# Routing arithmetic woven into the attention's maxima, GpSimd's biases regrouped, and a last group finished tile by tile

## The reference

```python
xn = layernorm(x)
q, k, v = split(xn @ w_qkv.T)                       # 2048 x 128 each
attn = (softmax(q @ k.T / sqrt(8)) @ v) @ w_proj.T + b_proj
t = xn @ W_in + b_in
topv, topi = top_k(softmax(t @ W_gate + b_gate), 2) # 8 experts, gates normalised to sum 1
moe = sum over the two experts: gate * (relu(t @ W1[e] + b1[e]) @ W2[e] + b2[e])
out = x + attn + (moe @ W_out + b_out)
```

## Time and profile before

| what | us |
|---|---|
| median of 3 runs | 242.5 |
| lowest and highest | 242.16, 242.7 |
| profiled execution, its own time | 242.35 |
| its span, first to last instruction | 240.6 |
| TensorE busy in the span | 226.1 (94%) |
| VectorE, ScalarE, GpSimd busy | 136.6, 111.7, 140.9 |

### The profile page before, as it was taken

How to read it: one execution, slowest core, us unless ns; L and a number is a source line. 1 busy time by engine, 2 the same in 40 slices (tenths; PEclk the granted TensorE clock), 3 DMA queues, 4 the chain that set the end, 5 groups by cost and what they waited for, 6 DMA issues and landing times.

```text
span 240.6 us, 4828 instructions
## 1 busy us (share of the span) xinstructions
PE 226.1 (94%) x1724; PEld 214.0 (89%) x1724; DVE 136.6 (57%) x330; ACT 111.7 (46%) x265; POOL 140.9 (59%) x163
## 2 busy tenths in 40 slices
PE   7699977999999999899999999999899999999983
PEld 7688865889999998899999999999899899999983
DVE  4978585364252551445444445444677886985642
ACT  2572520433524325354444554444656656567561
POOL 3149007888888820266555666553088888888610
PEclk9999999999999999999999999999999999999999
DMA  6799911101111121022222222221111113113201
GB/s 180 282 324 341 322 31 46 45 33 46 46 41 39 43 66 44 14 55 76 70 73 71 67 71 75 69 75 38 33 46 34 44 35 82 40 40 83 75 15 44
DMA packets 23047, 19.54 MB, mean 81 GB/s; under 512 B 3280, under 2 KB 19696, under 8 KB 22768
## 3 DMA queue, kind: packets, MB, share of 16 engines
q1 hardware_dynamic: 20000, 14.71, 20.1%
q0 software_dynamic: 2048, 4.20, 6.5%
q10 hardware_dynamic: 976, 0.33, 0.5%
HBM read 10.97 MB, written 8.26 MB: 80 GB/s over the span
## 4 chain that ended last, share of the span: by engine, by line
PE 78%; DVE 8%; DMA 4%; POOL 3%; issue 2%; ACT 1%; ACTq 1%; POOLq 0%; DVEq 0%
PE ps L1051 15%; PE ps L1037 15%; PE ps L917 10%; PE ps L853 6%; PE ps L792 5%; PE ps L793 5%; PE ps L794 5%; DVE part_max L601 3%; PE ps L926 2%; POOL wtab L380 2%; PE ps L930 2%; PE ps L927 2%; DMA w_raw<-in_L_attn_w_proj_dram 2%; PE ps L1025 2%; PE ps L800 2%
## 5 line engine op out<-in xcount | busy, mean ns | idle before, releaser
L343 POOL COPY wst<-wtab 128x1156 f32 x39 | 45.0, 1154 | 39.3 <-DVE y_sb L738 39.3
L454 ACT ACTIVATE pf<-ps 128x512 f32<-128x512 f32 x64 | 38.1, 595 | 36.5 <-PE ps L794 36.1
L601 DVE TENSOR_REDUCE part_max<-ps 128x1 f32<-128x1024 f32 x32 | 38.9, 1223 | 13.3 <-PE ps L853 13.1
L380 POOL DMA_INDIRECT wtab<-slots_out,slots x32 | 34.4, 1074 | 15.9 <-DMA slots_out<-y_sb 8.4
L353 POOL DMA_INDIRECT slots_in<-hl,slots x32 | 31.5, 985 | 18.7 <-DVE slots L677 11.7
L730 DVE TENSOR_SCALAR mid<-ps,wst 128x128 f32<-128x128 f32 x78 | 23.8, 347 | 32.5 <-PE ps L1037 32.5
L1051 PE MATMUL ps<-wst,mid 128*128 128x128 f32 x312 | 41.3, 275 | 0.7 <-DVE x_sb L628 0.7
L792 PE MATMUL ps<-q_hi,xnT_hi 128*128 128x256 f32 x128 | 41.2, 322 | 0.5 <-ACT q_hi L439 0.5
L1037 PE MATMUL ps<-xgT,wst 128*128 128x128 f32 x312 | 41.3, 275 | 0.0
L1051 PEld LDWEIGHTS ps<-wst,mid 128*128 128x128 f32 x312 | 38.0, 192 | 0.8 <-ACT mid L494 0.8
L1037 PEld LDWEIGHTS ps<-xgT,wst 128*128 128x128 f32 x312 | 38.0, 192 | 0.1
(11 more groups left out here) (145 smaller groups left out, 341.4 us busy)
## 6 DMA issues: line engine op xcount, KB each, us to landing
wtab<-in_L_ffn_W_dram SPq DMA_DIRECT2D x16, 256.0 KB, 5.9
xg<-slots_in SPq DMA_DIRECT2D x39, 64.0 KB, 2.0
slots_out<-y_sb SPq DMA_DIRECT2D x39, 64.0 KB, 1.5
slots_in<-wst SPq DMA_DIRECT2D x2, 1024.0 KB, 5.0
x_sb<-in_L_attn_x_dram SPq DMA_DIRECT2D x4, 256.0 KB, 4.9
out_dram<-x_sb SPq DMA_DIRECT2D x3, 256.0 KB, 2.6
wtab<-in_L_ffn_b_dram SPq DMA_DIRECT2D x1, 512.0 KB, 7.4
slots_in<-hl,slots POOLq DMA_INDIRECT x32
```

What stands on the lines that cost most here:

```text
L343: pool.tensor_copy(wst[:, t % 4, :], wtab[:, bass.ds(experts[t], 1), :].rearrange("p a n -> p (a n)")).then_inc(Z["staged"], 1)
L380: pool.indirect_dma_start(out=z[:, j, c, :], out_offset=None, in_=slots_out, in_offset=bass.IndirectOffsetOnAxis(ap=slots[:, c, j:j + 1], ...
L454: act.activation(pf[:, i % 3, :], ps[:, st_bank(i), :], ACT.Exp).then_inc(Z["pf_done"], 1)
L601: dve.tensor_reduce(part_max[:, g % 2, m // 2, m % 2:m % 2 + 1], ps[:, b:b + 2, :], AX.XY, ALU.max).then_inc(Z["max_read"], 1)
```

## The change

1. The last quarter of `hl` is copied by VectorE, behind `row_max(0)`, and counted on a semaphore of its own, for which `route_first` and TensorE's third score step wait.
2. The pairs of group 1 go to steps 2, 4, 5 and 6 of group 0. `route_slots` is cut in two: `route_bases` (totals to tile bases, eight instructions) at step 3, `route_slots` (four instructions) behind maximum 1 in step 4. So VectorE's order is maximum 0, bases, maximum 1, slots, maxima 2 and 3.
3. Nine tile biases ahead of the scatters, seven behind scatters 5, 7, ... 17.
4. The last group's end is written out per tile: the context is copied in two halves, each tile has its own output rows, scaling, projection and add; the MoE part of tiles 14 and 15 is multiplied first, into the banks onto which their projections are then accumulated; only tiles 12 and 13 get a separate MoE product (bank 4) and add (256 elements instead of 512).

```diff
-    PAIR_STEP = [[4, 5, 5, 6]] + 6 * [[1, 2, 4, 5]] + [[]]
+    PAIR_STEP = [[2, 4, 5, 6]] + 6 * [[1, 2, 4, 5]] + [[]]
-    BARE, UNTIED = 4, 2
+    UNTIED = 9
+    BIAS_AT = [5, 7, 9, 11, 13, 15, 17]
+        def row_bank(c):
+            return (MA, 0)[c]
+        def sum_bank(c):
+            return (MB, 1)[c]
...
-                if UNTIED + n - BARE in range(UNTIED, NT):
-                    bias(UNTIED + n - BARE)
+                if n in BIAS_AT:
+                    bias(UNTIED + BIAS_AT.index(n))
...
             row(0)
-            hl_copy(3)
...
+                parts = TILES[g] if g == NG - 1 else 1
+                for c in range(parts):
+                    w = n // NT // parts
+                    act.activation(to[:, :, w * c:w * (c + 1)], of[:, :, w * c:w * (c + 1)], ACT.Copy).then_inc(Z["ut_copied"], 1)
...
             def route_first():
-                dve.wait_ge(Z["hl_ready"], NR)
+                dve.wait_ge(Z["hl_ready"], NR - 1)
+                dve.wait_ge(Z["hl_last_ready"], 1)
...
             row_max(0)
+            dve.wait_ge(Z["hl_done"], NR)
+            dve.tensor_copy(hl[:, TB * (NR - 1):NT, :].rearrange("p (b j) n -> p b j n", b=2), hl_banks(NR - 1)
+                            ).then_inc(Z["hl_last_ready"], 1)
...
                 for k in range(STEPS[g]):
+                    if g == 0 and k == 3:
+                        route_bases()
                     for m in pairs_at(g, k):
                         pair_max(g + 1, m)
+                        if g == 0 and m == 1:
+                            route_slots()
...
-                    if g == 0 and k == 3:
-                        route_slots()
...
-            moe_add(NR - 1)
-            for r in range(ROUNDS[NG - 1]):
-                scale_out(NG - 1, r)
-            dve.wait_ge(Z["moe_added"], NR)
-            add_out(NG - 1).then_inc(Z["x_added"], 1)
+            def last_scale(c):
+                n = FIRST_ROUND[NG] - 1
+                dve.wait_ge(Z["out_done"], n + 1 + c)
+                link("rinv", dve.reciprocal(rinv[:, n % 2, c:c + 1], ps[:, row_bank(c), D:D + 1]))
+                dve.tensor_scalar(o_sb[:, n % 2, c, :], ps[:, row_bank(c), 0:D], rinv[:, n % 2, c:c + 1], None,
+                                  ALU.mult).then_inc(Z["o_ready"], 1)
+            def last_add(c):
+                at = x_sb[:, NT - 2 + c, :]
+                dve.wait_ge(Z["proj_done"], FIRST_ROUND[NG] + c)
+                return dve.tensor_tensor(at, ps[:, sum_bank(c), 0:D], at, ALU.add)
+            last_scale(0)
+            last_scale(1)
+            dve.wait_ge(Z["wo_done"], NR)
+            at = x_sb[:, NT - TB:NT - 2, :]
+            dve.tensor_tensor(at, ps[:, MX + 1, 0:2 * D].rearrange("p (j e) -> p j e", e=D), at, ALU.add).then_inc(Z["moe_added"], 1)
+            last_add(0)
+            last_add(1).then_inc(Z["x_added"], 1)
...
-            moe_project(NR - 1)
-            for r in range(ROUNDS[NG - 1]):
-                out_rows(NG - 1, r)
-                project(NG - 1, r)
+            for c in range(2):
+                at = P * (TB - 2 + c)
+                pe.matmul(ps[:, sum_bank(c), 0:D], cT[:, at:at + P], wo_sb[:, :], start=True, stop=False)
+            for c in range(2):
+                pe.wait_ge(Z["ut_copied"], NG + c)
+                pe.matmul(ps[:, row_bank(c), 0:D + 2], ut[:, P * c:P * (c + 1)], wvT[:, :], start=True, stop=True
+                          ).then_inc(Z["out_done"], 1)
+            pe.wait_ge(Z["moe_added"], NR - 1)
+            for j in range(TB - 2):
+                last = pe.matmul(ps[:, MX + 1, P * j:P * (j + 1)], cT[:, P * j:P * (j + 1)], wo_sb[:, :], start=True, stop=True)
+            last.then_inc(Z["wo_done"], 1)
+            for c in range(2):
+                n = FIRST_ROUND[NG] - 1
+                pe.wait_ge(Z["o_ready"], n + 1 + c)
+                pe.matmul(ps[:, sum_bank(c), 0:D], o_sb[:, n % 2, c, :], wpT[:, :], start=False, stop=True
+                          ).then_inc(Z["proj_done"], 1)
```

More of the change, by code:

```diff
@@ L185, in attention_moe_kernel @@
             xT_done xT_hi xT_lo xnn_hi_ready xnn_lo_ready x_biased
-            hl_done hl_ready route_link gap_ready e2_ready both_ready prefix_done prefix_read slots_ready experts_ready gates_ready
+            hl_done hl_ready hl_last_ready route_link gap_ready e2_ready both_ready prefix_done prefix_read slots_ready experts_ready gates_ready
             scattered
@@ L460, in copy_u @@
                     act.wait_ge(Z["out_done"], FIRST_ROUND[g])
-                act.activation(ut[:, 0:n].rearrange("e (p j) -> e j p", j=NT),
-                               ps[:, UB, 0:n].rearrange("e (j p) -> e j p", j=NT), ACT.Copy).then_inc(Z["ut_copied"], 1)
+                parts = TILES[g] if g == NG - 1 else 1
+                to = ut[:, 0:n].rearrange("e (p j) -> e j p", j=NT)
+                of = ps[:, UB, 0:n].rearrange("e (j p) -> e j p", j=NT)
+                for c in range(parts):
+                    w = n // NT // parts
+                    act.activation(to[:, :, w * c:w * (c + 1)], of[:, :, w * c:w * (c + 1)], ACT.Copy).then_inc(Z["ut_copied"], 1)
             def beside(g, k):
@@ L655, in route_second, with route_bases @@
                 dve.tensor_tensor(both[every], choice[:, 0, :, :], choice[:, 1, :, :], ALU.add).then_inc(Z["both_ready"], 1)
-            def route_slots():
+            below, total = [ps[:, MB, P * k:P * (k + 1)].rearrange("p (j e) -> p j e", e=NE) for k in (1, 2)]
+            def route_bases():
                 dve.wait_ge(Z["prefix_done"], 1)
-                below, total = [ps[:, MB, P * k:P * (k + 1)].rearrange("p (j e) -> p j e", e=NE) for k in (1, 2)]
                 flat = "p e j -> p (e j)"
@@ L671, in route_slots @@
                                                        scalar=float(SL), in1=cum[every], op0=ALU.mult, op1=ALU.add))
+            def route_slots():
                 dve.tensor_tensor(lg[every], below, cum[every].rearrange("p e j -> p j e"), ALU.add).then_inc(Z["prefix_read"], 1)
@@ L781, in _ @@
                         moe_add(BLOCK_AT[s - 1])
-            moe_add(NR - 1)
-            for r in range(ROUNDS[NG - 1]):
-                scale_out(NG - 1, r)
-            dve.wait_ge(Z["moe_added"], NR)
-            add_out(NG - 1).then_inc(Z["x_added"], 1)
+            def last_scale(c):
[8 more added lines that the diff above has]
+                return dve.tensor_tensor(at, ps[:, sum_bank(c), 0:D], at, ALU.add)
+            dve.wait_ge(Z["proj_done"], FIRST_ROUND[NG] - 1)
+            last_scale(0)
[5 more added lines that the diff above has]
+            last_add(1).then_inc(Z["x_added"], 1)
         @block.tensor
@@ L896, in scores @@
                 if i == 2:
-                    pe.wait_ge(Z["hl_ready"], NR)
+                    pe.wait_ge(Z["hl_last_ready"], 1)
                 if i >= base + 3:
@@ L1114, in _ @@
             values(LAST - 1)
-            moe_project(NR - 1)
-            for r in range(ROUNDS[NG - 1]):
-                out_rows(NG - 1, r)
-                project(NG - 1, r)
+            pe.wait_ge(Z["cT_copied"], NR)
+            pe.wait_ge(Z["x_added"], NG - 1)
+            pe.wait_ge(Z["pf_done"], LAST)
+            for c in range(2):
[14 more added lines that the diff above has]
+                          ).then_inc(Z["proj_done"], 1)
 _INS = ['L0_attn_x', 'L0_attn_w_qkv', 'L0_attn_w_proj', 'L0_attn_b_proj', 'L0_ffn_W_in', 'L0_ffn_b_in',
```

## The result

| | before | after |
|---|---|---|
| median (lowest to highest), us | 242.41 (242.16 to 242.70), 4 runs | 246.43 (245.59 to 248.96), 4 runs |
| profiled execution: time, span | 242.35, 240.6 | 247.15, 245.1 |
| row maximum of group 1 | 42.37 | 40.48 |
| last scatter starts | 85.06 | 84.80 |
| TensorE's first transpose of expert rows | 92.35 | 97.30 |

The ratio of the means is 1.0183 [1.0102, 1.0263]: the kernel became slower, and its median lies 6.8 us above the forecast and outside its range. The executions also scatter over 3.4 us, those of before over 0.5. A fifth execution, of 249.55 us, counts as slow by its distance to the fastest and is left out, though its granted clock, 0.986, is also that of the one of 248.96.

What follows compares the result with a forecast made beforehand. VectorE's sequence was taken as the bound from 26 to 42.6 us, with a second serial stretch at the end. Gains 2.8 - 0.5 + 0.6 = 2.9 us gave 239.6 us on the median, range 238.9 to 240.9.

Steps and rivals of the forecast that it cites:

- What the moved slots do to the scatters: GpSimd's scatters: slots 1.31 us later, seven biases fewer; 50.07 us become 47.4, slack 1.8, gain of 2.77 passes whole.
- three signs of failure: Expert transpose showing a wait, routing instructions stretched over 1.2 us in sum, or last store not following the last add.
- Scatters become the bound and the kernel slower: Rival, 4%: stretched scatter issues on GpSimd use up the slack and gain; 245.0 us if half were 0.45 longer.
- Scatters meet TensorE: Rival, 8%: removing seven biases shortens nothing, expert rows land 0.9 us late; gain 2.0, time 240.5.
- Port exclusion in full: Rival, 10%: four VectorE routing instructions each wait for a whole GpSimd bias; routing ends 1.6 us later, time 240.7.
- The interleave does nothing: Rival, 4%: pair 0 of group 1 not issued early enough, VectorE waits as before; 242.0 to 242.5 us.
- Copy of hl by VectorE: Before the routing: VectorE copies the last quarter in about 0.72 us, so routing arithmetic starts 0.42 earlier.
- Interleave: VectorE's routing stretch: group 1's maxima placed around the slot arithmetic; row maximum at 39.60 instead of 42.37, 2.77 earlier.
- Biases beside the routing: GpSimd's early biases beside VectorE's routing: four instructions lose 0.12 each, 0.5 us lost; bounds nothing and 1.2.
- Tail: Kernel's end, from the last context copy to the last store, split per tile: 0.6 us gained, bounds 0.3 and 0.75.

Runs made afterwards that it cites:

- bias: Kernel before with only the biases regrouped, nine ahead of the scatters and seven behind every second scatter from 5 on: 246.59 us, ratio 1.0172.
- bias_padded: Kernel before with the biases regrouped and an unused addition of the same shape behind scatters 4, 6 ... 16: 242.31 us, ratio 1.0002.
- routing: Kernel before with only parts 1 and 2 of the change; biases and tail as before: 240.49 us, ratio 0.9921.
- three_fewer: Whole change, but five biases ahead of the scatters and eleven behind scatters between 4 and 17: 239.41 us, ratio 0.9882.
- no_bias: Whole change, but biases as before, two ahead of the scatters and fourteen behind scatters 4 to 17: 240.37 us, ratio 0.9916.
- all_ahead: Kernel before with all sixteen biases ahead of the scatters and none between them: 268.63 us, ratio 1.1099.

## Why the prediction was wrong

**The failed step** is in *What the moved slots do to the scatters*: "fourteen stood there, seven remain, so the 50.07 us from the first scatter's start (35.96) to the last one's end (86.03) become 47.4". The arithmetic held (38.16 to 85.76 is 47.6), but the step booked a closer sequence of scatters as free of cost. The biases between them were also what kept the scatters apart. At 1.46 to 1.48 us ScalarE and VectorE begin up to 4.7 us behind TensorE's finished work, and since each score step, context and pair of maxima passes through such a hand-over, TensorE idles for 5.4 us between 43 and 93. Part 3 alone costs 4.3 us (bias less before on its chip), and the same part with the old period restored costs nothing (bias_padded). None of the three signs of failure that the prediction named came: the first expert transpose waits for no DMA, the routing is stretched by 0.5, and the last store follows the last add. The failure lay in a stretch of which it said only that it would begin earlier.

**Its rivals.** *Scatters become the bound and the kernel slower* had the sign and nearly the time (245.0), at 4%, but by another mechanism: stretched issues of GpSimd. They are not stretched, and the load of expert rows is not what TensorE waits for. *Scatters meet TensorE* describes the kernel without part 3: 1.15 us of waiting, 240.49 us against the 240.5 forecast, which also held the tail and the loss beside the biases, two terms that nearly cancel. Its own terms put the rows 0.8 late, not 0.9 (90.4 less 89.58). It was set aside rightly for the change itself. *Port exclusion in full* asked for 1.6 us beside the biases where 0.5 were lost, and *The interleave does nothing* is refuted by the row maximum 2.7 us earlier.

**What held.**
- *Copy of hl by VectorE*: 0.72 us as forecast. The routing began 0.33 us earlier than before without biases beside it (25.81 in routing), 0.42 forecast; 0.21 us between copy and first instruction were not counted, where 0.07 stood.
- *Interleave*: row maximum at 39.68 in routing and 39.64 in three_fewer, 2.7 us earlier; forecast 2.77. In "after" it is 40.48, by the 0.50 below and because the prologue ended 0.3 later in that execution (copy of hl at 25.18, in routing at 24.88).
- *Biases beside the routing*: two instructions 0.26 and 0.24 longer where four at 0.12 were forecast; 0.50 against 0.5. The number was right by two errors that cancel. The two ran beside biases 0.42 apart (3.82 / 9) and lost more than the 0.12 of the earlier trace rows and less than a whole bias. The Trainium skill (SBUF — State Buffer, Who interferes with whom) says that the one that issues first holds the shared port pair for its whole instruction and the other is blocked; the trace agrees with a wait for what is left of one bias, not with one for a whole bias each time, as the prediction's rival had it. The ninth bias ends at 27.41, and the other two instructions of that kind came behind it.
- *Tail*: 0.42 to 0.47 us against 0.6, within its bounds. The last add ends 2.92 us behind the start of the copy, against the 2.65 of the forecast. The copies are not the reason: the first half took 0.38 where 0.40 stood, and both end 0.60 behind the start where 0.70 stood. The mis-sized term is one tile's product with the wait before it: from the end of the first half copy to the end of the first output rows 0.55 us pass (235.28 to 235.83) where 0.43 stood, and from the end of the second scaling to the end of its projection again 0.55 (236.95 to 237.50) where 0.43 stood.

**The sum, corrected**: 2.7 for routing and maxima, 0.5 lost beside the biases, 0.4 for the tail. The kernels with parts 1 and 2 also spend about 0.3 us more outside their span, 2.1 us in the median of their executions against 1.8 in the others; the prediction carried the 1.8 of before over, and the cause isn't known. That makes 2.3 gained; 6.3 lost to lateness make the 4.0 us by which the median rose. The 6.3 are a remainder, not a measurement; after less no_bias, which has neither the 0.5 nor the lateness but waits 1.0 us for the expert rows, gives 6.1 + 1.0 - 0.5 = 6.6.

That late hand-overs from TensorE come from close scatters is shown: 33, 26, 19 and 3 to 9 us lost at periods of 1.20, 1.27, 1.36 and about 1.47 (each against the same kernel with the old biases; the first three and the 9 in part by a lower clock), no lateness in the profiled executions at 1.51 and above, and the padded run. Between the runs near 1.47 the loss differs more than their mean period explains. What on the chip is behind it is not shown.
## What to carry to other kernels

Work that looks like filler between GpSimd's indirect DMAs can be what spaces them; before taking it out, look at the mean period that remains (here 1.57 us cost nothing, 1.46 to 1.48 cost 3 to 9 us, 1.27 cost 26) rather than only at when the last one ends. When TensorE loses time and no engine, queue or transfer is named, compare the start of a waiting instruction with the end of what it waits for: a gap of microseconds where 0.1 is normal shows a late hand-over. And take out only as much as the slack asks for: three biases fewer were enough to meet TensorE, seven were not needed.

## What the runs showed of the hardware

- Indirect DMAs issued by GpSimd at a mean period of 1.48 us or less delay what ScalarE and VectorE learn of TensorE's results: an exponential was up to 26.8 us late at 1.20 (half rows), 17.0 at 1.27, 6.8 at 1.36, 4.7 at 1.48 and, where bare scatters followed one another, 7.1 at a mean of 1.46. At 1.51, 1.57 and 1.65 it was at most 0.1. ScalarE's and VectorE's results reach TensorE within 0.1 meanwhile (after, all_ahead). The semaphore's step itself is on record that late, and the waiting engine begins within 0.04 of it. The delay builds up over some eight scatters (all_ahead: scatters from 37.12 on, the first 0.6 of lateness at 47 us) and outlasts the dense part (there 10.6 at 77 us, none from 84 on, with weight copies between the scatters from 63.77).
- It does not depend on bytes (512 or 256 of each row: 268.63 and 267.68 us), and 64 rows instead of 128 shorten the issue from 0.97 to 0.89 us and make it worse (275.04).
- In "after", GpSimd's issues (0.95 to 0.99 us from 46 us on), VectorE's maxima (1.22 and 1.23) and TensorE's last products of a step (0.28) keep their lengths meanwhile, so no row of durations shows it.
